# Attention and gated feed-forward on one core: raw weight tiles split at other places, two fetches between write-backs, one rotation a period earlier

## The chip, the cores and the metric

The kernel runs on one core of a Trainium2 chip. The metric is the device time in microseconds of one execution. Engines are named as the profile names them: PE (TensorE; PEld is its weight load), DVE (VectorE), ACT (ScalarE), POOL (GpSimd) and SP (SyncE, which here issues most DMAs). A name with a q behind it, as SPq or ACTq, is the sequencer of that engine issuing a DMA.

## The reference

Four batches of 512 tokens, 512 channels, all float32. The whole is two residual steps:

```
x = x + attn(cond(x, f))        # cond: a two-way decayed scan over the tokens (bi-WKV), gated by x
x = x + ffn(cond2(x, f))        # the same with other decay; ffn: silu(z W1') * (z W3'), Hadamard, W2'
# attn: 16 heads of 128; in segments of 128 tokens: causal softmax(q k') v inside a segment,
# plus sigma(q) mem / (sigma(q) z) from a running memory with delta update, mixed by sigmoid(betas), then Wo
```

The Hadamard transform over the 2048 hidden units is applied to W2 instead (eight blocks), once, while attention runs.

## The kernel before

The attention part is one loop of 32 periods, `for n in range(NN)`, written out for each engine. Period n handles two heads (pair n % 8) of batch n // 8. So the first period is n = 0, the seventh n = 6, the ninth n = 8, the 30th and 31st n = 29 and 30. PE's order in a period is: transposes of the keys, scores, transposes of the output of period n - 1, then pieces of the projections for later periods set between the steps of period n's recurrent memory (`update`, `recall`, `turn_p`, `pv`). The projections are value blocks (`v_block`), used by `couple(n)`, and the keys and queries of period n + 1 (`kq_part`). Every fourth period (n = 4, 8, ...) is a burst that holds Wo (`wo`) besides. After the 32 periods comes the feed-forward, 32 units of `up` and `down`. Every float32 product is three fp32r matmuls (`three`), on high and low parts.

**Weight tiles.** Weights come in an order fixed by `weight_stream()` as numbered tiles, each 1024 columns of a high and 1024 of a low part, in a ring of seven slots (`parts`). ENDS[n] is the number of tiles asked for by the end of period n; ENDS is 4, 6, 10, 12, 24, 28, 32, 34, 46, 50 for n = 0 to 9. A tile that is met for the first time is raw. SP loads its two halves into two of four `stage` buffers (L2450), ACT makes the high part (`split_hi`, L1715) and POOL the low part (`split_w`, L2226); for the q tiles POOL makes both (L2224). `load_w`, `split_hi` and `split_w` take a tile number up to which they go, and all four engines take the calls in their own program order, so a call whose tile has not landed holds everything behind it on its engine. A stage buffer is loaded again when the tile before it in that buffer has been split. Most tiles are written back to HBM after the split (`keep`, L2479 and L2480, 512 KB each) and fetched later, ready (L2467, L2468, in `load_w`). A fetch into a slot waits until the slot's former tile is used, and, if that one was kept, until its write-back has landed (`wait_used`).

Tiles that matter here: 2, 3 = values for period 2 and 3, in n = 0 already; 4 = keys of period 2, 5 = its queries; 28 = keys of period 7, 29 and 30 = values for periods 8 and 9 (computed in period 6), 31 = queries of period 7, 32 = keys of period 8; 40 to 43 = o12 to o15, raw, for Wo of period 8; 44, 45 = keys and queries of period 9; 46, 47 = values computed in period 9, both fetched; 48, 49 = keys and queries of period 10. Tile 46 goes into the slot of tile 39, tile 47 into that of tile 40, tiles 48, 49 and 50 into those of 41, 42 and 43. Period 6 (SWAPPED) takes the first key part of the next period before its value blocks.

**Background steps.** The scans of `cond`, the Hadamard of W2 and so on are a list STEPS with costs, dealt by `shared_out()` to eight slots in each period. `behind(n, k)` on an engine runs its part of the steps of slots up to k. A step of the Hadamard is `load`, four levels `lv0` to `lv3` on DVE, `hi` (ACT, L1789, copies HA to HH), `lo` (DVE, L1246, HL = HA - HH), then `mult`, the rotation: four matmuls of 512 columns on PE (`hadamard`, L880 and L881), whose result ACT scales and sends to HBM (`out_w2`, L1807, L1809). A `mult` goes only into slots 1 to 3, at most one in a slot. PE reaches `behind` at k = 1 (after the first `update`) and k = 3 (after the first `recall`). The steps of the last blocks are dealt so in the kernel before: (29, 1) mult 5; (29, 2) hi 6, lo 6; (29, 3) load 7, lv0 7; (29, 4) lv1; (29, 5) lv2; (29, 7) lv3; (30, 1) mult 6; (30, 2) hi 7, lo 7; (30, 3) mult 7. ACT runs `out_w2(6)` after `hi` 7. The step yh of scan tile 7 (period 6, slot 2: ACT L1781, POOL L2251) completes the input y of batch 1, for which the value block of period 6 waits (`wait_y`).

The waits that gate a value block on PE:

```
if n == 0:
    w.wait_ge(a_qm, 2 + half + 1)          # ACT's relu of the queries of period 1, half
...
elif n == SWAPPED:
    w.wait_ge(a_km, 2 * (n + 1) + half + 1)
```

Of the kernel before, what the change touches and what calls it, by code (L numbers as in the profile page):

```python
# [65 lines left out]
STEPS = [(name, t, cost) for t in range(4, NA) for name, cost in SCAN]  # L66
STEPS += [("hstart", 0, 3000)]
for _i in range(8):
    for name, cost in HADAMARD:
        if name != "mult":  # L70
            STEPS.append((name, _i, cost))
        elif _i > 0:
            if _i == 2:
                STEPS += [(z, 0, c) for z, c in MODULATE[1:]]
            STEPS.append((name, _i - 1, cost))
            if _i == 1:
                STEPS.append(MODULATE[0][:1] + (0, 0))
# [75 lines left out]
SWAPPED = 6  # L153
# [157 lines left out]
def adaln_attn_ffn(nc, xT_d, fT_d, wu_d, wq_d, wk_d, wv_d, wo_d, betas_d,  # L311
# [9 lines left out]
    with ExitStack() as ctx:  # L321
# [1376 lines left out]
        def scalar(e):  # L1698
# [103 lines left out]
            def out_w2(i):  # L1802
                for j in range(2):
                    cut = slice(512 * j, 512 * j + 512)
                    w.wait_ge(pe_h, 2 * i + j + 1)
                    w.wait_ge(d_ho, 16 * i)
                    e.activation(HO[:, cut], X[j][:, :], ACT.Copy, scale=RSQ).then_inc(a_ho, 1)  # L1807
                w.wait_ge(a_ho, 2 * i + 2)
                e.dma_start(w2_s[i].rearrange("p a d -> p (a d)"), HO[:, :]).then_inc(d_ho, 16)  # L1809
# [10 lines left out]
            def behind(n, k):  # L1820
                for name, i, _ in STEPS[at[0]:UPTO[n, k]]:
                    if name == "nf":
                        load_k(i + 2 if i + 2 < NA else NT)
                    elif name == "er":
                        exp_r(i)
                    elif name == "ek":
                        exp_k(after(i))
                    elif name == "eu":
                        exp_u(after(i))
                    elif name == "rc1":  # L1830
                        load_r(i)
                    elif name == "yh":
                        high_y(i)
                        keep_ratio(i)
                    elif name == "hi":
                        high_w2(i)
                        if i == 7:
                            out_w2(6)
                    elif name == "load":
                        load_w2(i)  # L1840
                    elif name == "mult" and i != 6:
                        out_w2(i)
                    elif name == "zsig":
                        z_sigmoid(i)
                    elif name in ("z0", "z1", "z2", "z3"):
                        z_high(i, int(name[1]))
                at[0] = UPTO[n, k]
# [164 lines left out]
            for n in range(NN):  # L2012
                nx, burst = n + 1, is_burst(n)
# [21 lines left out]
                exp_s(n, 1)  # L2035
                behind(n, 1)
                if n in (SWAPPED, NN - 2):
                    copy_kq(nx, "k", 0, G[0])
                    exp_kq(nx, "k", 0, G[0])
                elif more and not bare:  # L2040
                    copy_v(n, 0)
                elif not more:
                    sigmoid(0, 0, G[0])
# [3 lines left out]
                    exp_u(4)  # L2047
                if burst:
                    copy_v(n, 1)
                if n == SWAPPED:  # L2050
                    behind(n, 3)
                split_hi(o + 3 if burst else 3 if n == 0 else end if more else end + 1)
                behind(n, 3)
                if n == SWAPPED:
# [34 lines left out]
                        copy_kq(nx, "k", j, G[j])  # L2089
                        exp_kq(nx, "k", j, G[j])  # L2090
                if more:
                    split_hi(5 if n == 0 else end + (3 if n == 3 else 1 if burst else 2))
                    copy_kq(nx, "q", 0, G[0])
                    exp_kq(nx, "q", 0, G[0])
                    if n not in (0, 4):
                        split_hi(end + (4 if n == 3 else 3 if burst else 2))
                    copy_kq(nx, "q", 1, G[1])
                    if n == 0:
                        exp_kq(nx, "q", 1, G[1])
                    if n == 4:  # L2100
                        split_hi(end + 3)
                else:
                    high_h(0, 0)
                    high_h(0, 1)
# [100 lines left out]
        def gpsimd(e):  # L2205
# [133 lines left out]
            for n in range(NN):  # L2339
# [10 lines left out]
                if n == 0:  # L2350
                    ekv(4)
                    euv(4)
                if n == SWAPPED:
                    behind(n, 3)
                split_w(o + 3 if burst else 3 if n == 0 else end if more else end + 1)
                behind(n, 3)
                if burst:
# [11 lines left out]
                if burst:  # L2369
                    split_w(end + 2)  # L2370
                if more:
                    split_w(5 if n == 0 else end + (4 if n == 3 else 3 if burst else 2))
                else:
                    low_h(0, 0)
                    low_h(0, 1)
# [50 lines left out]
        def sync(e):  # L2426
# [110 lines left out]
            for n in range(NN):  # L2537
# [27 lines left out]
                keep(o + 5 if burst else end + 2 if n == 3 else end)  # L2565
                load_w(o + 9 if burst else 6 if n == 0 else end + (5 if n == 3 else 3))
                behind(n, 5)
                if burst:
                    keep(o + 8)
                    load_w(o + 11)  # L2570
# [5 lines left out]
                    load_w(o + 13)  # L2576
                if more:
                    keep(5 if n == 0 else end + (4 if n == 3 else 2 if burst else 1))
                    load_w(end + (6 if n == 3 else 4))
                behind(n, 7)  # L2580
            def load_x(b):
                w.wait_ge(d_x1[b], 16)
# [107 lines left out]
```

## Time and profile before

| | us |
|---|---|
| median of 3 runs (lowest, highest) | 1588.19 (1587.49, 1588.75) |
| profiled execution, device time | 1588.17 |
| its span | 1586.4 |
| PE busy | 1543.0, 97% |
| DVE busy | 1227.3, 77% |
| ACT busy | 780.6, 49% |
| POOL busy | 614.5, 39% |
| DMA, 42.4% of 16 engines on SP's queue | 276.58 MB |
| mean granted clock of TensorE | 0.997 |

The profiled execution lies 0.02 us under the median, and its time is 1.8 us more than its span. The attention loop starts at 60.71 us of the span and its 32nd period at 1044.61.

### The profile page before, as it was taken

Reading aid. Unit: us, or ns where it says so; the run is one execution under the profiler, and the core shown is the slowest. Engines: PE = TensorE matmul, PEld = TensorE weight load, DVE = VectorE, ACT = ScalarE, POOL = GpSimd, SP = SyncE. Lnnn points to the kernel's source line nnn. Section 1 sums busy time; section 2 is a strip of 40 time slices with the busy share of each in tenths; the row PEclk is TensorE's granted clock in tenths of the full one; section 3 lists DMA queues with packets and bytes.
Section 4 is the critical chain, followed back from the end, with each engine's and each line's share of the span. In section 5 each row is a group of like instructions: output and inputs, shape, how many; then the busy total and the mean of one; then the engine's idle time right before and its main releaser. Section 6 shows DMA issues by size and latency. Waiting matters only on the chain.

```text
span 1586.4 us, 24552 instructions
## 1 busy us (share of the span) xinstructions
PE 1543.0 (97%) x8406; PEld 1323.7 (83%) x8406; DVE 1227.3 (77%) x2746; ACT 780.6 (49%) x1687; POOL 614.5 (39%) x433
## 2 busy tenths in 40 slices
PE   4899999999999999999999999999999999999999
PEld 2678998888888888888888888888888888888887
DVE  8869967897788788888775774666897888687785
ACT  3556655645526535644555562663554443344442
POOL 3647656361211113221101010143664465666662
PEclk9999999999999999999999999999999999999999
DMA  5356677578485387386278658347211122311111
GB/s 176 122 194 242 242 280 255 190 267 316 156 309 186 108 294 246 103 316 236 84 261 338 222 196 311 114 166 260 88 58 54 58 88 74 106 43 64 54 41 54
DMA packets 113405, 276.58 MB, mean 174 GB/s; under 512 B 11648, under 2 KB 36608, under 8 KB 111872
## 3 DMA queue, kind: packets, MB, share of 16 engines
q1 hardware_dynamic: 94416, 241.96, 42.4%
q10 hardware_dynamic: 18864, 33.04, 6.8%
q8 instruction: 68, 1.11, 0.3%
q14 instruction: 57, 0.47, 0.1%
HBM read 226.71 MB, written 48.25 MB: 173 GB/s over the span
## 4 chain that ended last, share of the span: by engine, by line
PE 89%; DVE 5%; issue 2%; ACT 1%; POOL 1%; DMA 1%; SPq 0%; ACTq 0%; POOLq 0%; DVEq 0%
PE psG L664 14%; PE psG L666 14%; PE psG L665 13%; PE psG L788 5%; PE psX L860 3%; PE psX L664 3%; PE psX L666 3%; PE psX L665 3%; PE psX L815 3%; PE psG L790 3%; PE psZ L841 3%; PE psZ L832 2%; PE psZ L666 2%; PE psY L666 2%; PE psZ L665 2%
## 5 line engine op out<-in xcount | busy, mean ns | idle before, releaser
L2226 POOL TENSOR_TENSOR parts<-stage,parts 128x512 fp32r<-128x512 f32 x160 | 234.4, 1487 | 145.2 <-ACT parts L1715 142.9
L664 PE MATMUL psG<-yh,parts 128*128 128x512 f32 x646 | 263.0, 407 | 0.1
L666 PE MATMUL psG<-yh,parts 128*128 128x512 f32 x646 | 253.1, 392 | 0.0
L665 PE MATMUL psG<-yl,parts 128*128 128x512 f32 x646 | 251.9, 390 | 0.0
L2294 POOL TENSOR_TENSOR vs<-v,omb 128x512 f32<-128x512 f32 x64 | 92.0, 1460 | 387.0 <-PE psX L815 209.6
L666 PEld LDWEIGHTS psG<-yh,parts 128*128 128x128 f32 x646 | 121.2, 188 | 26.7
L664 PEld LDWEIGHTS psG<-yh,parts 128*128 128x128 f32 x646 | 121.7, 188 | 22.0 <-issue 0.9
L665 PEld LDWEIGHTS psG<-yl,parts 128*128 128x128 f32 x646 | 121.8, 189 | 21.5
L788 PE MATMUL psG<-heads,parts 128*128 128x512 f32 x384 | 135.5, 394 | 0.0
L1715 ACT ACTIVATE parts<-stage 128x512 fp32r<-128x512 f32 x152 | 87.9, 623 | 56.7 <-DMA stage<-in_w 16.6
L1875 ACT ACTIVATE kT<-psG 128x512 f32<-128x512 f32 x62 | 36.9, 595 | 149.9 <-PE psG L666 148.5
L664 PE MATMUL psG<-parts,yh 128*128 128x512 f32 x240 | 101.8, 424 | 7.8 <-ACT etmp L1893 3.7
L790 PE MATMUL psG<-heads,parts 128*128 128x256 f32 x384 | 108.2, 282 | 0.0
L1220 DVE RECIPROCAL DBK<-DF 128x128 f32<-128x128 f32 x120 | 107.3, 926 | 0.6
L1923 ACT ACTIVATE S<-S,st 128x128 f32<-128x128 f32 x256 | 99.0, 391 | 7.7 <-issue 5.5
L1303 DVE CUSTOM_DVE_ANT_0 S<-psX,mask 128x128 f32<-128x128 f32 x256 | 57.9, 286 | 55.5 <-PE psX L815 55.4
L1315 DVE TENSOR_TENSOR mem<-psZ,mem 128x129 f32<-128x129 f32 x192 | 47.8, 287 | 66.1 <-PE psZ L832 66.1
L666 PE MATMUL psG<-parts,yl 128*128 128x512 f32 x240 | 95.6, 399 | 0.0
L665 PE MATMUL psG<-parts,yh 128*128 128x512 f32 x240 | 94.4, 393 | 0.0
L2302 POOL TENSOR_TENSOR hl<-sg,hh 128x512 fp32r<-128x512 f32 x36 | 51.0, 1416 | 91.0 <-ACT hh L1973 91.0
L788 PEld LDWEIGHTS psG<-heads,parts 128*128 128x128 f32 x384 | 72.1, 188 | 14.7
L1884 ACT ACTIVATE etmp<-etmp 128x512 f32<-128x512 f32 x126 | 79.5, 632 | 3.9
(281 smaller groups left out, 4146.3 us busy)
## 6 DMA issues: line engine op xcount, KB each, us to landing
parts<-high_o SPq DMA_DIRECT2D x52, 512.0 KB, 6.0
parts<-low_o SPq DMA_DIRECT2D x52, 512.0 KB, 7.5
parts<-high_v SPq DMA_DIRECT2D x36, 512.0 KB, 5.2
parts<-low_v SPq DMA_DIRECT2D x36, 512.0 KB, 6.4
stage<-in_w SPq DMA_DIRECT2D x64, 256.0 KB, 3.1
parts<-high_k SPq DMA_DIRECT2D x23, 512.0 KB, 5.6
parts<-low_k SPq DMA_DIRECT2D x23, 512.0 KB, 7.0
parts<-high_q SPq DMA_DIRECT2D x23, 512.0 KB, 4.9
```

The lines of the kernel that those rows point to most:

```text
L664: e.matmul(out, lh, rh, start=first, stop=False, skip_group_check=check)
L665: e.matmul(out, lh, rl, start=False, stop=False, skip_group_check=check)
L666: return e.matmul(out, ll, rh, start=False, stop=last, skip_group_check=check)
L788: e.matmul(out[:, :], hi[:, cols], heads[:, :, 8 * half + r, :], start=half == 0 and r == 0, stop=last_row, skip_group_check=True)
L790: k = e.matmul(out[:, 0:256], lo[:, cols], heads[:, 0, 8 * half + r, :], start=False, stop=last_row, skip_group_check=True)
L1220: e.reciprocal(dbk[:, 128 * j:128 * j + 128], df[:, 128 * j:128 * j + 128]).then_inc(v_rc, 1)
L1303: m = e.tensor_tensor_reduce(S[:, j, seg(s)], X[j][:, seg(s)], mask[:, :], -SCALE, -NEG, ALU.add, ALU.min, st[:, 1, j, s:s + 1])
L1715: e.activation(hi, raw, ACT.Copy).then_inc(a_wh, 1)
L1884: e.activation(below(n, kind, j), below(n, kind, j), ACT.Exp, scale=-1.0).then_inc(a_ke if kind == "k" else a_qe, 1)
L1923: m = e.activation(S[:, j, seg(s)], S[:, j, seg(s)], ACT.Exp, bias=st[:, 1, j, s:s + 1], scale=-1.0, accum_out=st[:, 2, j, s:s + 1])
L2226: e.tensor_tensor(lo, raw, hi, ALU.subtract).then_inc(p_wl, 1)
L2294: e.tensor_tensor(vs[:, :, j, :].rearrange("p (a b) d -> p a b d", a=2), pick(v[:, :, :, j, 0:P], *HALVES[n]), omb[:, 128 * j:128 * j + 12 ...
```

## The change

1. n = 0, ACT: `split_hi(5)` (tile 4) stands behind the copies and exponentials of the queries of period 1, no longer ahead of them.
2. n = 5: ACT and POOL also split tile 30 at the end of the period (`end + 3` for `end + 2`), and SP also loads tile 32 there (`end + 5` for `end + 4`). They did the one inside period 6's softmax (`end - 1`) and the other at the start of period 6.
3. n = 6 and n = 30, ACT: `behind(n, 2)` runs ahead of the copy and the exponential of the next keys, not behind them. In n = 6 `behind(n, 3)` no longer stands ahead of the split of tile 31, on ACT and POOL.
4. n = 8, SP: the fetches of tiles 46 and 47 are set between the write-backs: write back 40, fetch 46, write back 41, fetch 47, write back 42 and 43. Before, 40 to 43 were written back and then 46 and 47 fetched.
5. Rotation 6 is one period up. The list now deals: (29, 3) mult 6; (29, 4) load 7, lv0 7; (29, 5) lv1; (29, 6) lv2; (29, 7) lv3; (30, 1) nothing; (30, 2) hi 7, lo 7; (30, 3) mult 7. `out_w2(6)` runs with it, in (29, 3).

```diff
--- before.py
+++ after.py
@@ -66,10 +66,12 @@
 STEPS = [(name, t, cost) for t in range(4, NA) for name, cost in SCAN]
 STEPS += [("hstart", 0, 3000)]
 for _i in range(8):
+    if _i == 7:
+        STEPS.append(("mult", 6, 300))
     for name, cost in HADAMARD:
         if name != "mult":
             STEPS.append((name, _i, cost))
-        elif _i > 0:
+        elif 0 < _i < 7:
             if _i == 2:
                 STEPS += [(z, 0, c) for z, c in MODULATE[1:]]
             STEPS.append((name, _i - 1, cost))
@@ -1834,11 +1836,9 @@
                         keep_ratio(i)
                     elif name == "hi":
                         high_w2(i)
-                        if i == 7:
-                            out_w2(6)
                     elif name == "load":
                         load_w2(i)
-                    elif name == "mult" and i != 6:
+                    elif name == "mult":
                         out_w2(i)
                     elif name == "zsig":
                         z_sigmoid(i)
@@ -2035,6 +2035,7 @@
                 exp_s(n, 1)
                 behind(n, 1)
                 if n in (SWAPPED, NN - 2):
+                    behind(n, 2)
                     copy_kq(nx, "k", 0, G[0])
                     exp_kq(nx, "k", 0, G[0])
                 elif more and not bare:
@@ -2047,8 +2048,6 @@
                     exp_u(4)
                 if burst:
                     copy_v(n, 1)
-                if n == SWAPPED:
-                    behind(n, 3)
                 split_hi(o + 3 if burst else 3 if n == 0 else end if more else end + 1)
                 behind(n, 3)
                 if n == SWAPPED:
@@ -2089,16 +2088,17 @@
                         copy_kq(nx, "k", j, G[j])
                         exp_kq(nx, "k", j, G[j])
                 if more:
-                    split_hi(5 if n == 0 else end + (3 if n == 3 else 1 if burst else 2))
+                    if n > 0:
+                        split_hi(end + (3 if n == 3 else 1 if burst else 2))
                     copy_kq(nx, "q", 0, G[0])
                     exp_kq(nx, "q", 0, G[0])
                     if n not in (0, 4):
-                        split_hi(end + (4 if n == 3 else 3 if burst else 2))
+                        split_hi(end + (4 if n == 3 else 3 if burst or n == 5 else 2))
                     copy_kq(nx, "q", 1, G[1])
                     if n == 0:
                         exp_kq(nx, "q", 1, G[1])
-                    if n == 4:
-                        split_hi(end + 3)
+                    if n in (0, 4):
+                        split_hi(5 if n == 0 else end + 3)
                 else:
                     high_h(0, 0)
                     high_h(0, 1)
@@ -2350,8 +2350,6 @@
                 if n == 0:
                     ekv(4)
                     euv(4)
-                if n == SWAPPED:
-                    behind(n, 3)
                 split_w(o + 3 if burst else 3 if n == 0 else end if more else end + 1)
                 behind(n, 3)
                 if burst:
@@ -2369,7 +2367,7 @@
                 if burst:
                     split_w(end + 2)
                 if more:
-                    split_w(5 if n == 0 else end + (4 if n == 3 else 3 if burst else 2))
+                    split_w(5 if n == 0 else end + (4 if n == 3 else 3 if burst or n == 5 else 2))
                 else:
                     low_h(0, 0)
                     low_h(0, 1)
@@ -2565,6 +2563,10 @@
                 keep(o + 5 if burst else end + 2 if n == 3 else end)
                 load_w(o + 9 if burst else 6 if n == 0 else end + (5 if n == 3 else 3))
                 behind(n, 5)
+                if n == 8:
+                    load_w(o + 11)
+                    keep(o + 6)
+                    load_w(o + 12)
                 if burst:
                     keep(o + 8)
                     load_w(o + 11)
@@ -2576,7 +2578,7 @@
                     load_w(o + 13)
                 if more:
                     keep(5 if n == 0 else end + (4 if n == 3 else 2 if burst else 1))
-                    load_w(end + (6 if n == 3 else 4))
+                    load_w(end + (6 if n == 3 else 5 if n == 5 else 4))
                 behind(n, 7)
             def load_x(b):
                 w.wait_ge(d_x1[b], 16)
```

## Rows read from the trace of the kernel before

**Rows 1.** Waits of PE, whole span (total us, times, longest us):
```profile
PE psG L664 <- ACT etmp L1893: 3.7, 1, 3.7
PE psG L664 <- POOL yl L2251: 2.5, 1, 2.5
...
PE psG L664 <- issue: 1.7, 1, 1.7
...
PE psX L880 <- DVE HL L1246: 1.3, 1, 1.3
```

**Rows 2.** Busy time by stretch, one period each (us, PE, PEld, DVE, ACT, POOL, clock):
```profile
60.71:93.18 32.47, 27.82 (x151) 23.30 (x151) 20.73 (x59) 18.84 (x46) 25.13 (x21) 0.95 0.64 214
93.18:119.26 26.08, 26.08 (x160) 22.95 (x158) 20.57 (x63) 16.67 (x41) 9.71 (x8) 1.00 0.39 137
248.47:278.91 30.44, 27.95 (x159) 24.12 (x158) 22.23 (x63) 16.55 (x41) 18.04 (x15) 0.94 0.78 276
353.54:381.53 27.99, 26.34 (x160) 23.02 (x159) 22.21 (x65) 15.63 (x39) 6.90 (x5) 1.00 0.99 390
993.58:1020.61 27.03, 27.03 (x164) 23.75 (x163) 19.50 (x62) 16.05 (x39) 2.56 (x2) 1.00 0.38 135
```

**Rows 3.** The same view of two short stretches:
```profile
87.30:90.70 3.40, 3.40 (x10) 2.62 (x9) 0.00 (x0) 1.36 (x3) 1.84 (x3) 0.50 1.01 346
356.90:358.70 1.80, 0.14 (x3) 0.06 (x1) 1.80 (x11) 1.56 (x6) 0.05 (x1) 1.00 1.04 418
```

**Rows 4.** Timeline of PE at two waits inside the loop (start, us, what, idle before):
```profile
81.95 0.39 PE L666 MATMUL psG<-yh,parts 128*128 128x512 f32 x1
86.02 0.47 PE L664 MATMUL psG<-parts,yh 128*128 128x512 f32 x1 [3.68 <-ACT etmp L1893]
...
261.31 0.72 PE L664 MATMUL psG<-parts,yh 128*128 128x512 f32 x1 [2.49 <-POOL yl L2251]
```

**Rows 5.** Timeline of ACT, end of the first period:
```profile
83.23 0.63 ACT L1715 ACTIVATE parts<-stage 128x512 fp32r<-128x512 f32 x1 [5.00 <-DMA stage<-in_wk]
84.27 0.63 ACT L1715 ACTIVATE parts<-stage 128x512 fp32r<-128x512 f32 x1 [0.41 <-DMA stage<-in_wk]
...
85.28 0.59 ACT L1893 ACTIVATE etmp<-psG 128x512 f32<-128x512 f32 x1
```

**Rows 6.** Timelines of ACT and of POOL in the seventh period:
```profile
254.48 1.14 ACT L1715 ACTIVATE parts<-stage 128x512 fp32r<-128x512 f32 x2
...
257.07 0.57 ACT L1875 ACTIVATE kT<-psG 128x512 f32<-128x512 f32 x1
...
258.69 0.61 ACT L1781 ACTIVATE yh<-OY 128x512 fp32r<-128x512 f32 x1
...
259.38 1.68 POOL L2251 TENSOR_TENSOR yl<-OY,yh 128x512 fp32r<-128x512 f32 x1 [0.64 <-ACT yh L1781]
```

**Rows 7.** SP in the ninth period: an issue, its waits, landing of L2468 at 343.53:
```profile
343.17 0.32 SPq L2467 DMA_DIRECT2D parts<-high_v  x1
...
SPq L2467 <- DMA low_o<-parts: 7.0, 4, 2.5
...
DMA to landing us min/median/max: 15.1/15.1/15.1
```

**Rows 8.** Timelines of PE, DVE and ACT, 30th and 31st period:
```profile
1003.21 0.47 PE L664 MATMUL psG<-parts,yh 128*128 128x512 f32 x1
...
1003.81 1.22 DVE L1246 TENSOR_TENSOR HL<-HA,HH 128x1024 fp32r<-128x1024 f32 x1 [3.04 <-ACT HH L1789]
...
1027.73 0.58 ACT L1875 ACTIVATE kT<-psG 128x512 f32<-128x512 f32 x1
...
1029.37 1.04 ACT L1789 ACTIVATE HH<-HA 128x1024 fp32r<-128x1024 f32 x1
...
1030.44 1.23 DVE L1246 TENSOR_TENSOR HL<-HA,HH 128x1024 fp32r<-128x1024 f32 x1 [2.65 <-ACT HH L1789]
...
1031.77 0.47 PE L880 MATMUL psX<-HH,had 128*128 128x512 f32 x1 [1.28 <-DVE HL L1246]
```

## The prediction

> **What bounds the kernel now.** I read the page's busy times first: PE works for 97% of the span, so only two things can move the end, PE's work or PE's waits. The edits add and remove no work on any engine; they move it. So next come PE's waits. Inside the loop there are four of more than 1 us [rows 1], and the change has a part for each: 3.7 us for ACT's relu of the queries, 2.5 for a low part of y from POOL, 1.7 that the profile can't name, and 1.3 for HL from DVE. Then I cut the loop into periods. An ordinary one takes 26.08 us, all of it PE; the first, seventh and ninth take 32.47 (with other work in it), 30.44 and 27.99 [rows 2]. The seventh is 4.36 longer but idle for 2.5 only. The rest is the clock: after the long idle stretch of the first period PE was granted 0.50, the 1.2 GHz level, for 3.4 us [rows 3], and matmuls of 512 columns that are otherwise 0.23 us apart (the pace of the whole timeline) come 0.43 apart; the seventh period has the same, mean clock 0.94 [rows 2]. The 1.66 us wait at 357 us did not lower it, 1.00 all through [rows 3]. After the loop the change touches nothing.
>
> **First period (part 1).** PE's last query matmul starts at 81.95, the first of the value block at 86.02 [rows 4]. It waited for the relu at 85.28, 0.59 long [rows 5]. ACT was idle for 5.00 us before that, in its program order stuck at the split of tile 4, whose halves land at 83.2 and 84.3 [rows 5]. The queries of head 0 were ready at about 79.7 (12 matmuls of 0.23 before PE's end). After the change ACT takes copy and relu then and is done by 81, before PE gets there at 82.18; head 1's relu is done by 83.5, while PE needs it 12 matmuls later, at 84.9. Gain: 86.02 - 82.18 = 3.84, and of the half-clock stretch half of 3.4 = 1.7, together 5.5. What is late instead: tile 4's split starts at about 84.0 rather than 83.23, so its low part on POOL is 0.8 later. It is used only in the middle of period 1, over 10 us later. With the cover gone (if POOL's later split of tile 5 then held period 1's queries) it would cost what POOL is late, 0.8.
>
> **Seventh period (parts 2 and 3).** PE's wait ends with yl, 259.38 + 1.68 = 261.06 on POOL, 0.25 before PE's start at 261.31 [rows 4, 6]. yl waits for yh, which ACT starts at 258.69, and ahead of yh stand, in this period, the split of tile 30 (1.14 of two, 1.05 net) and the copy, relu and exponential of the next keys, 258.69 - 257.07 = 1.62 [rows 6]. Both leave: yh starts at 258.69 - 1.05 - 1.62 = 256.02, ends 256.63; POOL, without tile 30's 3.5 us, starts yl at 256.71 and ends by 258.39, and PE may go at 258.64. PE's natural start is 261.31 - 2.49 - 0.17 (the modelled overlap) = 258.65. So the wait goes just to nothing. The keys' relu, which this block also needs, ends at about 257.7. Gain: all that this period has over an ordinary one, 30.44 - 26.08 = 4.36 [rows 2], idle and half clock. The split goes to the end of period 5, on ACT between the two heads' queries, where its 1.05 us delays the second copy by 0.15, and on POOL behind tile 29, well before yh. SP's extra load waits there for POOL's low part of tile 30, and the write-back of tile 29 is queued behind it, some 2.5 us later; nobody needs that slot before period 8. Bounds: 0.5 less if yl is late again, nothing more.
> The Trainium skill (SBUF — State Buffer, "SBUF: two separate sides") says that a VectorE operation with two SBUF inputs and a GpSimd one that reads SBUF exclude each other for a whole instruction. By it yl, moved beside a scan, would wait for that scan; the sum would be 0.5 smaller. The row's 1.68 for yl is already such a slow one, so the sum above stands by the row.
>
> **Ninth period (part 4).** PE starts again at 358.67; the fetch of tile 47's low half is issued at 343.53 and lands 15.1 later, at 358.63 [rows 7]. That is the unnamed wait. SP issued this fetch at 343.17, just when the write-back of tile 40 had landed (its waits are of this kind, 7.0 us of four) [rows 7]. From then on ten halves land in 15.5 us: six of write-backs 41 to 43, two of tile 46, two of 47, so 1.55 each at a full DMA (share 1.04) [rows 3]. After the change tile 47 still can't be issued before 343.17, but ahead of it are only 41 and 46: six halves, 9.3 us, landing at 352.5. PE needs it at 358.67 - 1.66 - 0.17 = 356.8. Gain: 27.99 - 26.08 = 1.91 [rows 2]. Late instead: write-backs 42 and 43, and behind them tiles 48 to 50; the keys (48) stay the 11th and 12th halves, 343.1 + 18.6 = 361.7, needed at 353.54 + 10.1 = 363.6 (in an ordinary period those keys' first matmul lies 10.1 in). Cover is thin, 1.9 us.
>
> **Rotation (part 5, and part 3 in n = 30).** Here the change pays. In (29, 3) PE has finished the recall and starts its next work at 1003.21 [rows 8]. Rotation 6 now stands there, and it needs HL of block 6, which DVE makes from 1003.81 to 1005.03, right behind ACT's HH, and neither moves [rows 8]. With the 0.1 us that PE took after HL at 1031.67 [rows 8], PE starts at 1005.12: a new wait of 1.9. The rotation's own work, about 27.03 - 26.08 = 0.95 [rows 2], only changes its period. In period 30 HL of block 7 held PE until 1031.77; the natural start, at the same place as 1003.21 in its period (9.63 after 993.58), is 1020.61 + 9.63 = 1030.24, so 1.53 is lost now. After the change HH starts at 1027.73, without the keys' 1.64 ahead of it, HL ends 1.04 + 0.02 + 1.23 later at 1030.02, PE could go at 1030.12, but it arrives 0.95 earlier, at 1029.29: 0.83 is still lost. Net: 1.91 - 1.53 + 0.83 = +1.21. Levels of block 7 are one slot later; the one in slot 6 puts DVE's sigma of the keys about 1 us nearer to the next period, with 2 us of room. ACT's wait for the w2 write ahead of its second output goes, and hides nothing for PE.
>
> **Sum.** -5.5 - 4.4 - 1.9 + 1.2 = -10.6 on the span of 1586.4: 1575.8. The device time of this execution is 1.8 above its span, 1588.17, at the median of 1588.19. I predict 1577.5, by 0.67% faster. Its own range is 1576.5 to 1578.5.
>
> **Rivals.**
> - *The new wait in period 29 lowers the clock.* Idle 1.7 us there is as long as the wait at 357 us that left it at 1.00 [rows 3], against it. For it: two longer ones did lower it. Price half of 3.4 = 1.7, time 1579.2. The Trainium skill (TensorE: Matmul & The Clock Gate, "What's actually happening") says that the gate goes by how busy the engine has lately been; by it either level is possible, which is why this has a chance.
> - *The rotation finds HL ready*, if ACT or DVE come to hi 6 and lo 6 sooner than the rows show. Then 1.9 of the sum goes: 1575.6. Nothing in the diff moves them, against it.
> - *The seventh period keeps part of its wait.* yl is ready at PE's natural start to within 0.01. If ACT is held at tile 30 in period 5, or yl starts late, idle and perhaps the clock come back: 0.5 to 4.4, time 1578 to 1581.9.
> - *The early gain is given back.* PE comes to periods 1 to 3 5.5 us sooner, and DVE, POOL (25.13 of 32.47 busy) or a load may not be [rows 2]. Against: ACT and POOL idle in period 1, POOL busy 9.71 of 26.08. Time up to 1583.
> - *The parts do nothing*: the relu is not what held PE, tile 47 isn't either. Against: both releases fit to 0.2 us. Time 1588.2.
> - *Slower: SP stands still at tile 47.* In period 8 everything behind (42, 43, 48, 49, 50) waits for one write-back. If its landing slips, tile 48 lands after 363.6 and PE stalls in period 9. To lose more than the other parts gain (8.7 without the 1.9, and 3.2 more to be slower by 0.2%), it would have to land at 363.6 + 8.7 + 3.2 = 375.5, 13.8 later than worked out. Nine more halves would do that. Time 1591.4 and up.
>
> **Chances.** Main case 0.60, clock 0.11, HL ready 0.08, seventh period 0.08, given back 0.06, nothing 0.04, slower 0.03. A difference under 0.2%, 3.2 us, is about what a measurement of this kernel can't tell from none. The range 1575.0 to 1582.0 takes in the first four, 0.87. Faster by over 0.2% (below 1585.0): the first five, 0.93; within: 0.04; slower: 0.03.
>
> **What the profile after would show.** In the first period no wait of PE for ACT's etmp, and clock 1.00 where it was 0.50; period length near 26.9. In the seventh, L2251 at about 248 + 8.2 after the shift of 5.5, no wait, 26.1 long. In the ninth, 26.1 long, fetch of tile 47 landing 4 us ahead of use, SP's L2467 between L2479 and L2480 pairs. In the 30th, PE waiting about 1.7 idle for DVE HL L1246, the period 29.9 long; in the 31st, another of 0.6, 22.3 long instead of 24.0. I would be wrong if one of the three large gains is matched by a longer period next to it, or if the clock falls at a place where it didn't.

## The result and the profile after

The changed kernel takes 1578.13 us (median of 6 runs, 1577.67 to 1582.11), the kernel before 1587.84 beside it (6 runs, 1585.40 to 1588.75). The ratio is 0.9945, with a 95% interval of 0.9933 to 0.9958: faster by 0.4 to 0.7%. The prediction was 1577.5.

The first profiled execution was the longest of the six. TensorE was granted 0.95 of full speed in nearly all of it. So I also read a second one, from the run `after_again` below: 1578.28 us, clock 0.998. Both pages, first and second execution; the columns are busy us, share of the span and instructions:

```profile
span 1580.3 us, 24552 instructions
...
PE 1544.1 (98%) x8406; PEld 1326.8 (84%) x8406; DVE 1227.1 (78%) x2746; ACT 780.9 (49%) x1687; POOL 614.9 (39%) x433
```

```profile
span 1576.4 us, 24552 instructions
...
PE 1539.6 (98%) x8406; PEld 1321.4 (84%) x8406; DVE 1228.8 (78%) x2746; ACT 780.5 (50%) x1687; POOL 614.9 (39%) x433
```

Everything below reads the second, whose clock is like that of before. Its span is 9.93 below the 1586.4 of before. First PE's waits, as in [rows 1] (us in total, times, longest):

```profile
...
PE psX L882 <- issue: 2.3, 2, 1.7
PE psG L679 <- DVE qT L1208: 1.6, 1, 1.6
PE psZ L842 <- DVE mem L1317: 1.3, 4, 0.5
```

The four waits of [rows 1] are gone from the list. In their place stand two of the rotation (L882 is L880 of before; PE's lines are two further down), 1.7 and 0.6, and one of 0.5 for `mem`. Then the periods, as in [rows 2]: first, second, seventh, ninth, 30th and 31st (us, PE, PEld, DVE, ACT, POOL, clock, DMA share, GB/s):

```profile
60.42:87.33 26.91, 25.95 (x151) 22.25 (x151) 20.77 (x60) 19.10 (x46) 21.40 (x17) 1.00 0.55 192
87.33:114.16 26.83, 26.35 (x160) 22.91 (x159) 21.35 (x63) 16.66 (x41) 13.81 (x12) 1.00 0.60 203
243.38:269.48 26.10, 26.10 (x160) 22.99 (x159) 22.13 (x63) 15.85 (x40) 17.62 (x15) 1.00 0.84 285
344.16:370.26 26.10, 26.10 (x160) 22.99 (x159) 22.14 (x65) 15.52 (x39) 6.87 (x5) 1.00 1.02 401
982.26:1012.08 29.82, 28.14 (x168) 24.56 (x167) 19.44 (x62) 17.13 (x41) 2.56 (x2) 1.00 0.41 139
1012.08:1034.43 22.35, 21.76 (x140) 19.31 (x139) 15.68 (x54) 16.75 (x41) 8.06 (x6) 1.00 0.13 36
```

Lengths before and after, with the difference: first 32.47, 26.91 (-5.56); second 26.08, 26.83 (+0.75); seventh 30.44, 26.10 (-4.34); ninth 27.99, 26.10 (-1.89); 30th 27.03, 29.82 (+2.79); 31st 24.00, 22.35 (-1.65). Together -9.90 of the -9.93. The windows are cut at PE's first matmul of each period. The period that the prediction calls the ninth, at 353.54 in before, is that of n = 9, the tenth if one counts from the first. It is called the ninth here too. SP issues the transfers for it in the period ahead of it, n = 8.

The first period, ACT's rows against [rows 5] and PE's against [rows 4]:

```profile
79.84 0.59 ACT L1893 ACTIVATE etmp<-psG 128x512 f32<-128x512 f32 x1
...
83.95 1.24 ACT L1717 ACTIVATE parts<-stage 128x512 fp32r<-128x512 f32 x2
```

```profile
81.66 0.39 PE L668 MATMUL psG<-yh,parts 128*128 128x512 f32 x1
81.89 0.39 PE L666 MATMUL psG<-parts,yh 128*128 128x512 f32 x1
```

The relu is done at 80.4, and PE goes from the last query matmul to the value block with the usual 0.23 between. The split of tile 4 now starts at 83.95.

The seventh, ACT and POOL against [rows 6]:

```profile
250.96 0.61 ACT L1783 ACTIVATE yh<-OY 128x512 fp32r<-128x512 f32 x1
251.48 0.57 ACT L1875 ACTIVATE kT<-psG 128x512 f32<-128x512 f32 x1
```

```profile
251.65 1.32 POOL L2251 TENSOR_TENSOR yl<-OY,yh 128x512 fp32r<-128x512 f32 x1 [4.31 <-ACT yh L1783]
```

The step yh lies 7.6 us into the period, where it was 10.2, ahead of the copy of the keys, and yl follows with 1.32 rather than 1.68. A scan of DVE was still going when yl began:

```profile
250.67 1.21 DVE L1169 TENSOR_TENSOR_SCAN DF<-dec,EK 128x512 f32<-128x512 f32 x1
```

SP in n = 8, against [rows 7] (SPq L2465 and L2466 are fetches, L2477 and L2478 write-backs):

```profile
323.77 0.55 SPq L2477 DMA_DIRECT2D high_o<-parts  x1
...
325.20 0.65 SPq L2465 DMA_DIRECT2D parts<-high_v  x1
...
326.73 0.66 SPq L2477 DMA_DIRECT2D high_o<-parts  x1
...
333.88 0.32 SPq L2465 DMA_DIRECT2D parts<-high_v  x1
...
334.91 0.42 SPq L2477 DMA_DIRECT2D high_o<-parts  x1
...
339.29 0.32 SPq L2465 DMA_DIRECT2D parts<-high_k  x1
```

In order: write-back 40, fetch 46, write-back 41, fetch 47, write-backs 42 and 43, fetch 48. The halves of tile 47 land at 340.06 and 341.92. PE comes to the value block at about 347.4, 5.5 later.

The rotation in the 30th and the 31st period, PE and DVE, against [rows 8]:

```profile
991.76 0.39 PE L843 MATMUL psZ<-mem,sq 128*128 128x129 f32 x2
993.82 0.47 PE L882 MATMUL psX<-HH,had 128*128 128x512 f32 x1 [1.68 <-issue]
...
1021.62 0.47 PE L882 MATMUL psX<-HH,had 128*128 128x512 f32 x1 [0.59 <-issue]
```

```profile
992.50 1.22 DVE L1248 TENSOR_TENSOR HL<-HA,HH 128x1024 fp32r<-128x1024 f32 x1 [3.04 <-ACT HH L1791]
```

HL ends at 993.72 and PE starts 0.10 later. The profile calls it "issue", but the end of HL fits; rotation_hi_early below tests it.

### The profile page after: what moved, and what is told of

It is laid out like the page before. It is cut to its first block, busy times and chain, and to the rows that moved or that the text cites. A ratio compares the mean times of both kernels' runs of the same rounds, so it can differ in the third digit from the quotient of the medians.

```text
span 1580.3 us, 24552 instructions
## 1 busy us (share of the span) xinstructions
PE 1544.1 (98%) x8406; PEld 1326.8 (84%) x8406; DVE 1227.1 (78%) x2746; ACT 780.9 (49%) x1687; POOL 614.9 (39%) x433
## 3 DMA queue, kind: packets, MB, share of 16 engines
q8 instruction: 68, 1.11, 0.3%
## 4 chain that ended last, share of the span: by engine, by line
PE 91%; DVE 5%; issue 2%; ACT 1%; POOL 0%; DMA 0%; ACTq 0%; SPq 0%; DVEq 0%; POOLq 0%
PE psG L666 14%; PE psG L668 14%; PE psG L667 14%; PE psG L790 6%; PE psX L862 4%; PE psX L666 3%; PE psX L668 3%; PE psX L667 3%; PE psX L817 3%; PE psG L792 3%; PE psZ L843 3%; PE psZ L834 3%; PE psZ L842 2%; PE psZ L668 2%; PE psY L668 2%
```

## The experiments

Theory A is the prediction's: five parts worth -5.5, -4.4, -1.9 and, for the rotation with its order on ACT, +1.2, which add up because they lie in different periods. Its rivals: the rotation costs nothing or its wait isn't HL's; the parts don't add up; and, once the trace of after was read, the second period's 0.75 belongs to something else than part 1. All times are medians in us where there were more runs, with the profiled span and the lengths of the periods n = 0, 1, 6, 9, 29 and 30:

| kernel | time (runs) | span | 0 | 1 | 6 | 9 | 29 | 30 |
|---|---|---|---|---|---|---|---|---|
| before | 1587.88 (13) | 1586.4 | 32.47 | 26.08 | 30.44 | 27.99 | 27.03 | 24.00 |
| after_again | 1578.40 (4) | 1576.4 | 26.91 | 26.83 | 26.10 | 26.10 | 29.81 | 22.35 |
| no_rotation | 1576.13 (4) | 1574.3 | 26.91 | 26.62 | 26.10 | 26.10 | 27.03 | 22.95 |
| rotation_only | 1590.85 (10) | 1590.3 | 33.73 | 26.11 | 30.45 | 27.96 | 29.82 | 23.97 |
| rotation_hi_early | 1578.12 (1) | 1576.3 | 26.90 | 26.59 | 26.10 | 26.10 | 29.37 | 22.36 |
| first_only | 1582.42 (1) | 1580.6 | 26.89 | 26.67 | 30.46 | 27.70 | 27.03 | 24.03 |
| fetch_only | 1582.71 (1) | 1580.9 | 30.84 | 26.07 | 28.85 | 26.10 | 27.03 | 24.02 |
| split_only | 1586.62 (1) | 1584.8 | 32.88 | 26.09 | 27.45 | 27.47 | 27.03 | 24.01 |
| order_only | 1584.12 (1) | 1582.3 | 32.44 | 26.07 | 27.73 | 27.75 | 27.03 | 22.95 |
| rotations_later | 1576.08 (4) | 1574.2 | 26.90 | 26.61 | 26.10 | 26.10 | 27.03 | 22.96 |
| rotation_later_29 | 1577.32 (1) | 1575.5 | 26.89 | 26.60 | 26.10 | 26.10 | 27.93 | 22.35 |
| before_look1 | 1587.54 (1) | 1585.7 | 32.39 | 26.08 | 28.85 | 28.16 | 27.03 | 23.99 |
| before_look2 | 1590.08 (1) | 1588.3 | 32.63 | 26.07 | 30.42 | 29.89 | 27.03 | 24.00 |

The periods of "before" are those of the trace shown ahead of the prediction; its 13 runs were made beside the first four experiments, the second to fifth row (1585.73 to 1590.39). The four single parts had one run of before beside them (1587.49), the last four rows seven (median 1586.48, 1585.29 to 1591.13). A single time can't tell parts of 1 to 3 us from the spread of before, so the single parts are judged by their periods.

**after_again.** The changed kernel as it is.

> The changed kernel as it is, run again. Its first profiled execution was granted a clock of 0.949 all through and took 1582.1 us, while five others took 1577.7 to 1578.8 at 0.996 to 0.998. Theory: the 0.949 belongs to that execution and not to the kernel, so this profile has 1.00 again, a span near 1576.2, periods of 26.1 us (not 26.25), the 30th period near 29.8 and the 31st near 22.3. Rival: the changed kernel is throttled now and then because TensorE is busier; then 0.95 shows again here.

Measured: 1578.40 (1578.28 to 1578.55), ratio 0.9933 (0.9918 to 0.9948), clock 0.998 or 0.999 in all four runs. So the long first execution is not what the kernel usually does. It is one of ten of the changed kernel. The rival, that the change makes such an execution likelier, is neither borne out nor excluded by these runs.

**no_rotation.** Without part 5, all else as after.

```diff
-    if _i == 7:
-        STEPS.append(("mult", 6, 300))
...
-        elif 0 < _i < 7:
+        elif _i > 0:
...
                         high_w2(i)
+                        if i == 7:
+                            out_w2(6)
...
-                    elif name == "mult":
+                    elif name == "mult" and i != 6:
```

> The changed kernel with its part 5 undone: rotation 6 is back in the 31st period, while ACT still copies HH ahead of the next keys there. Theory (the rotation put one period up costs 1.2 us, and the earlier HH is what helps): the 30th period is 27.0 us without a wait for HL, the 31st 22.5 with a wait of at most 0.2, since HL ends at 9.4 into the period and PE reaches rotation 7 at 9.6. Together 49.5 for 52.4 in the changed kernel: 2.9 us less, 1575.2 us in all. Rival (the rotation put up is what removes the wait in the 31st period): the wait of 1.3 there comes back, the two periods take 51.0 and the time is 1.4 us less than the changed kernel's; if moving it up was a gain by itself, the time is above 1578.

Measured: 1576.13 (1575.95 to 1577.04), ratio to before 0.9920 (0.9905 to 0.9935), 2.3 below after_again on the same chip. Period 29 is 27.03 again, and period 30 is 22.95, not the 22.5 that I expected. The timeline of ACT has the reason, and PE's the rest (start, us, what, idle before and who ended it):

```profile
1017.06 1.06 ACT L1789 ACTIVATE HH<-HA 128x1024 fp32r<-128x1024 f32 x1 [0.47 <-PE psX L881]
```

```profile
1019.48 0.47 PE L880 MATMUL psX<-HH,had 128*128 128x512 f32 x1 [0.24 <-DVE HL L1246]
```

There is one HH. Its copy for block 7 has to wait until rotation 6, in the same period, has read it. Moving rotation 6 out of period 30 frees HH sooner and takes PE's work with it, which is worth 0.60 there (22.95 against 22.35). But it costs 2.79 in period 29.

**rotation_only.** Part 5 alone on the kernel before (the same lines the other way round).

> The kernel before with part 5 alone. Theory: the 30th period gets the wait for HL of block 6, idle 1.7 us, and is 29.9 long; in the 31st PE comes 0.95 earlier to rotation 7 while HL of block 7 still stands behind the keys on ACT, so it ends as late in the period as before and the period stays near 24.0 with a wait of 2.2. Sum 53.9 for 51.0: 2.9 us slower than before, 1590.9 us. Clock 1.00 in both waits, or 1.7 more if a 2.2 us wait lowers it. Rival (the rotation alone is worth its part): not slower than before.

Measured: 1590.85 (1589.96 to 1595.26), ratio 1.0021 (1.0011 to 1.0030): slower by 3.0. Period 29 is 29.82 as in after, and period 30 gains nothing (23.97): without part 3, ACT's HH still comes behind the keys, so PE, earlier by the rotation's work, only waits longer:

```profile
1035.10 0.47 PE L882 MATMUL psX<-HH,had 128*128 128x512 f32 x1 [2.21 <-issue]
```

The shorter period 30 of after needs both parts, and the -1.65 there is mostly part 3's: order_only alone has 22.95.

**rotation_hi_early.** In period 29 ACT makes HH of block 6 ahead of a copy of values, so that HL, and nothing else of PE's, comes earlier.

```diff
                 elif more and not bare:
+                    if n == 29:
+                        behind(n, 2)
                     copy_v(n, 0)
```

> The changed kernel, and in the 30th period ACT makes HH of block 6 ahead of the copy of a value block (0.5 us) instead of behind it. Theory (PE waits there for HL, that is for ACT's HH): the wait falls by 0.5, from 1.67 to about 1.2, the period from 29.8 to 29.3. Rival (PE waits for the bank or for the output of rotation 5, or for nothing that moves): 29.8 as in the changed kernel.

Measured: PE's wait is 1.20 instead of 1.68, and the period 29.37 instead of 29.81.

```profile
993.26 0.47 PE L882 MATMUL psX<-HH,had 128*128 128x512 f32 x1 [1.20 <-issue]
```

PE's wait moves with HL, by 0.48, while PE's own work before it stays. So what the profile calls "issue" is HL, as the prediction had it.

**first_only, fetch_only, split_only, order_only.** One part each on the kernel before, in this order: part 1; part 4; part 2; part 3.

```diff
-                    split_hi(5 if n == 0 else end + (3 if n == 3 else 1 if burst else 2))
+                    if n > 0:
+                        split_hi(end + (3 if n == 3 else 1 if burst else 2))
...
-                    if n == 4:
-                        split_hi(end + 3)
+                    if n in (0, 4):
+                        split_hi(5 if n == 0 else end + 3)
```

```diff
+                if n == 8:
+                    load_w(o + 11)
+                    keep(o + 6)
+                    load_w(o + 12)
```

```diff
-                        split_hi(end + (4 if n == 3 else 3 if burst else 2))
+                        split_hi(end + (4 if n == 3 else 3 if burst or n == 5 else 2))
...
-                    load_w(end + (6 if n == 3 else 4))
+                    load_w(end + (6 if n == 3 else 5 if n == 5 else 4))
```

(the first of these also in `split_w` for POOL)

```diff
                 if n in (SWAPPED, NN - 2):
+                    behind(n, 2)
                     copy_kq(nx, "k", 0, G[0])
...
-                if n == SWAPPED:
-                    behind(n, 3)
```

(the second of these also for POOL)

> The kernel before with part 1 alone (ACT splits tile 4 behind the queries of period 1). Theory: the first period falls from 32.47 to 26.8 us, with no stretch at clock 0.50 behind it, the periods 1 to 5 keep their lengths, time 5.6 us less, 1582.4. Rival (the gain is given back): one of the next periods grows by as much as PE comes early, up to 5.5 us in all.

> The kernel before with part 4 alone (fetches of tiles 46 and 47 between the write-backs). Theory: the ninth period's follower, n = 9, falls from 27.99 to 26.1 us; tile 47 is still asked for only at 343.2, when the write-back of tile 40 has landed, but lands at about 352.5 rather than 358.6. Time 1.9 us less. Rival (the DMA engines are full, so later transfers are late instead): PE waits in the same period for the keys, tile 48, and the period stays above 27.

> The kernel before with part 2 alone (tile 30 split and tile 32 loaded one period earlier). Theory: in the seventh period (n = 6) yh still stands behind the keys on ACT but 1.05 us earlier, at about 257.6; yl ends at about 260.0 and PE goes at 260.2, 1.6 us late instead of 2.65; the idle time is then 1.4, too short to lower the clock. The period is 27.7 us for 30.44. Rival (all of the wait goes already with the tile off POOL): 26.1. Rival (the tile was not in the way): 29.4 or more.

> The kernel before with part 3 alone (background steps ahead of the keys' copy in n = 6 and n = 30). Theory for n = 6: ACT starts yh at about 257.07, but POOL is at the low part of tile 30 until 258.74 and makes yl then, to 260.4; PE goes at 260.7, 2.0 us late, idle 1.85, clock 1.00; the period is 28.1 us. For n = 30: HL of block 7 is there before PE, the wait of 1.3 goes, the period falls from 24.0 to 22.5. Rival: yl waits for more than ACT's order, and n = 6 stays above 29.

first_only: period 0 is 26.89 and period 1 26.67 instead of 26.08, the others as before but for the ninth, 27.70, whose wait varies. (The time, 1582.42, is the 1582.4 expected by luck: the expectation had no give-back, and the loop of this execution started 0.68 earlier.) So the give-back in period 1 belongs to part 1. PE's longer period 1 has one place. In the second trace of after its matmuls lie as before, to 0.01, up to the end of the first `update`'s projections; the first `recall` starts 0.63 later in the period, ends 0.11 later still, and all that follows stays 0.75 behind. PE, DVE and POOL there:

```profile
95.86 0.49 PE L842 MATMUL psZ<-mem,sk 128*128 128x129 f32 x2 [0.48 <-DVE mem L1317]
```

```profile
90.82 1.47 DVE L1375 SCALAR_TENSOR_TENSOR sq<-qT,etmp 128x512 f32<-128x512 f32 x1
92.22 1.28 DVE L1361 TENSOR_TENSOR heads<-psY,heads 128x512 fp32r<-128x512 f32 x2
93.42 0.68 DVE L1375 SCALAR_TENSOR_TENSOR sq<-qT,etmp 128x512 f32<-128x512 f32 x1
94.02 0.41 DVE L1143 TENSOR_SCALAR EK<-kx 128x512 f32<-128x512 f32 x1
94.35 1.27 DVE L1195 TENSOR_TENSOR_SCAN NBK<-dec,last,NF 128x512 f32<-128x512 f32 x1
95.54 0.46 DVE L1317 TENSOR_TENSOR mem<-psZ,mem 128x129 f32<-128x129 f32 x2
```

```profile
90.45 1.29 POOL L2226 TENSOR_TENSOR parts<-stage,parts 128x512 fp32r<-128x512 f32 x1
```

DVE goes from 90.82 to `mem` without a gap, so what makes its first step longer makes PE late. That step, sq, took 1.47, its twin at 93.42 0.68. In before this step took 0.69. There the same POOL instruction ended at 93.30, 3.4 ahead of sq; here it ends at 91.74, with sq begun. In six traces with part 1 the long sq (1.25 to 1.47) ends 0.55 after that POOL instruction, each time: 92.29 after 91.74, 91.74 after 91.19, 92.11 after 91.55. A step slowed by sharing would not end so. It stood still until POOL was done. PE's loss follows it: in these six traces sq is 0.56 to 0.78 longer than in before, and the period, each time, 0.02 to 0.05 less than that. By the Trainium skill (SBUF — State Buffer, "SBUF: two separate sides") a VectorE operation with two SBUF inputs and a GpSimd one that reads SBUF hold their port one at a time; the trace agrees here. I didn't run a kernel that takes POOL's split away from there, so that the 0.6 to 0.8 of sq is what reaches PE rests on the rows.

fetch_only: period 9 is 26.10, all of part 4's 1.89. But periods 0 and 6 are 1.6 shorter than before, with PE's waits still there. This was unexpected, and before_look1 and before_look2 below are there to explain it. By the other traces without part 4 in which the clock stays up there (27.47 to 28.16), it is worth 1.4 to 2.1.

split_only and order_only: either alone leaves a wait of PE in the seventh period, 1.11 and 1.40, and a period 1.35 and 1.63 longer than an ordinary one. The clock stayed at 1.00 there. POOL's rows, split_only and order_only:

```profile
258.69 1.27 POOL L2251 TENSOR_TENSOR yl<-OY,yh 128x512 fp32r<-128x512 f32 x1 [5.98 <-ACT yh L1781]
```

```profile
255.22 3.46 POOL L2225 TENSOR_TENSOR parts<-stage,parts 128x512 fp32r<-128x512 f32 x2 [5.35 <-ACT parts L1715]
258.65 1.26 POOL L2250 TENSOR_TENSOR yl<-OY,yh 128x512 fp32r<-128x512 f32 x1
```

In split_only yl waits for ACT, which had the keys first. In order_only ACT is in time, but POOL is held by tile 30. Each of the two parts takes one of them away. Both periods are shorter than expected (27.7 and 28.1), in order_only by what yl is shorter: no scan was ahead of it, and it took 1.26 and not the 1.68 of before. Period 30 of order_only is 22.95 and not 22.5, for the reason found in no_rotation.

**rotation_later_29.** After, with the rotation of period 29 twelve projection matmuls later on PE.

```diff
                 recall(n, 1)
-                behind(n, 3)
+                if n != 29:
+                    behind(n, 3)
...
+                if n == 29:
+                    behind(n, 3)
                 turn_p(n)
```

> The changed kernel, and in the 30th period PE does rotation 6 behind 12 more matmuls of the projections (2.8 us later in its order). Theory (the cost of part 5 is only the place, where HL isn't there): no wait, the period is 27.03 + 0.95 = 28.0 for 29.8, the 31st as before at 22.35, time 1.8 less than the changed kernel, 1576.5. Rival (two rotations in a period cost more than their matmuls, through the bank or through the output's wait for HO): PE waits elsewhere in the period, which stays above 28.5.

Measured: period 29 is 27.93, and PE has no wait at the rotation (994.87, right behind 994.64). So the +2.79 of period 29 is the rotation's work, 0.9, and 1.88 of waiting for HL. The time of this one run, 1577.32, is 1.1 below after_again and not 1.9: its loop starts 0.4 later (60.85 for 60.42), and what follows the loop took 492.7 rather than 491.9.

**rotations_later.** no_rotation, with the second rotation of period 30 behind `turn_p` on PE.

```diff
-                behind(n, 3)
+                if n != NN - 2:
+                    behind(n, 3)
...
                 turn_p(n)
+                if n == NN - 2:
+                    behind(n, 3)
```

> The version without part 5 (1576.1 us), and in the 31st period PE does rotation 7 behind the transposes of the scores instead of ahead of them. In that version the period is 22.95 us and PE still waits 0.5 for HL, since ACT's HH of block 7 has to wait until rotation 6 has read the one before. Theory: with 0.9 us of other work in front, the wait is covered and the period is 22.5; 0.45 less in all, 1575.7, which is under what the medians can tell. Rival: ACT's output of the rotation now stands in front of its copy of the transposed scores at the wrong time, PE waits for that instead, and the period stays at 22.95 or grows.

Measured: 1576.08 (1575.25 to 1576.39), ratio 0.9931 (0.9912 to 0.9950), period 30 22.96: nothing gained. My theory, that the wait for HL was all that period 30 had left to give, fell. PE now stands a little later for ACT:

```profile
1023.65 1.60 PE L860 MATMUL psX<-vs,pT 128*128 128x128 f32 x12 [0.24 <-ACT pT L1934]
```

The wait of 0.24 for HL in no_rotation is one of 0.24 for the transposed scores here.

**before_look1, before_look2.** The kernel before, unchanged, twice.

> The kernel before, for its granted clock. In its first trace the clock fell to half for 3.4 us behind both long waits; in the trace with part 4 alone the same two waits were 3.6 and 2.5 us long and the clock did not fall, the periods were 30.84 and 28.85 us instead of 32.47 and 30.44. Theory: the fall is drawn anew in each execution and is worth 1.6 us each time, so the periods are one or the other of these values, and the spread of this kernel's times (1585.4 to 1590.4) holds it. Rival: part 4 itself kept the clock up; then this run has both falls, 32.5 and 30.4.

> The same kernel once more, a second draw: by the theory either value in each of the two periods, by the rival 32.5 and 30.4 again.

PE's clock behind the waits; first fetch_only (behind the wait of the first period, 3.65, and of the seventh, 2.51), then before_look1 (behind 3.64 and 2.50), then before_look2 (behind the 1.94 of the ninth):

```profile
85.50:89.00 3.50, 3.50 (x15) 2.88 (x16) 0.00 (x0) 2.64 (x5) 1.33 (x3) 1.00 0.92 363
259.20:262.60 3.40, 3.40 (x21) 3.00 (x22) 0.64 (x4) 1.09 (x2) 3.23 (x4) 1.00 1.03 401
```

```profile
85.80:89.20 3.40, 3.40 (x9) 2.64 (x10) 0.00 (x0) 2.54 (x5) 1.15 (x3) 0.50 0.93 364
261.10:264.50 3.40, 3.40 (x21) 2.99 (x22) 0.69 (x5) 1.09 (x2) 3.23 (x4) 1.00 0.99 386
```

```profile
360.10:363.40 3.30, 3.30 (x10) 2.62 (x10) 0.00 (x0) 1.69 (x7) 0.62 (x1) 0.50 1.02 394
```

With the clock at 1.00 PE gets 15 to 21 instructions done in 3.4 us, at 0.50 nine or ten. The same wait of the same kernel is followed by the 1.2 GHz level in one execution and not in another. In the seven traces that have the first period's wait of 3.6 to 4.1, the clock fell behind it in six (not in fetch_only). Of the six with the seventh's 2.5, it fell in four (not in fetch_only and before_look1). Each fall makes its period 1.6 longer: 30.44 against 28.85 in the seventh, 32.47 against 30.84 in the first.

## Why the prediction was right, and where it was off

**First period.** -5.5 predicted, -5.56 measured. PE goes straight on, the split of tile 4 starts at 83.95 (84.0 predicted). The 3.9 of it that is idle stretch is saved in every execution; the 1.6 of the clock only in those in which it would have fallen.

**Seventh.** -4.4, measured -4.34, no wait. "The wait goes just to nothing" had the value of yl at 1.68; it took 1.32, and yh came at 7.6 where I had 7.55. Both parts are needed for it. The prediction weighed at 0.5 that yl has to stand still for a scan of DVE. It does, and it costs almost nothing here: yl ended 1.09 after the scan (251.88), and as the scan had only 0.23 left, that made 1.32 of it. In before the scan had 0.6 left, and yl ended 1.06 after it, with 1.68; without a scan ahead it takes 1.26 or 1.27 (order_only, split_only). So the row's 1.68 was the slow case, as the prediction said.

**Ninth.** -1.9, measured -1.89. Tile 47 is 5.5 ahead of its use (4.3 predicted, from 1.55 a half), SP went on with tile 48 when 41's write-back had landed, and 48 was in time: its halves landed by 351.51, PE needs them 10.1 into the period, at about 354.3. The slower rival did not come.

**Rotation.** +1.2, measured +1.14: +2.79 in the 30th (1.9 and 0.95 predicted, 1.88 and 0.9 measured), -1.65 in the 31st (-1.53 + 0.83 - 0.95 = -1.65 predicted). The clock did not fall at this wait, in after_again nor at the 2.21 in rotation_only. Against the kernel that has all other parts the rotation costs 2.3, more than the 1.2, as part of what period 30 gains comes from part 3 alone.

**The term that was mis-sized** is the give-back, which the sum had at nothing: "against: ACT and POOL idle in period 1". It was 0.75 (0.5 to 0.75 in the traces with part 1). The prediction looked at how busy POOL is over period 1, 9.71 of 26.08, and not at where: POOL's last work of period 0 came only 1.6 us sooner (90.45 for 92.01) while PE came to period 1 5.85 sooner, so it slid into the first 4.5 us of period 1, where one DVE step needs the same port. The rival had the right sign and place and 0.06 of the chance; its price was small enough to leave the forecast standing. The 0.8 that the prediction names as its cover for this part is near the 0.75 by chance: that was for POOL's split holding period 1's queries, which did not happen.

**The sum.** Predicted -10.6 on the span, measured -9.93; the 0.75 explains it. The time came out at 1578.13 (1578.40 in the second set) for 1577.5.

**Treated as certain, and not so:** the 1.7 each for the clock in the first and seventh period. They were in this execution of before, so the sum against it is right. But before has executions without them. That fits its spread, 1585.29 to 1591.13, against 0.3 for the four of after_again and 1.1 for the first six without the long one. Without the two falls its span would be 1586.4 - 1.6 - 1.6 = 1583.2 and the gain 6.8; against before_look2, with all three falls, it is 11.9. A part of what this change gives is that the waits behind which the clock may fall are gone. That the forecast came within 0.6 us rests in part on luck: the execution it was read from had two of the three falls and lay at the median of its set.

**The best version** is no_rotation: parts 1 to 4 without the fifth, 1576.13, 0.8% below before, and 2.3 below the change as made. rotations_later, 1576.08 in other company, is by its periods not different from it.

## What to carry to other kernels

Price each edit in the period where its wait ends last, and then look at what the neighbours of that period had going on at that moment of time, not over the period: work that doesn't move with the bottleneck engine slides against it. Moving a unit of work of the bound engine forward is free only if its operands are there: compare the end of the producer with the new place, row by row, and, where they don't fit, put the unit behind other ready work (rotation_later_29) or leave it. A part of a change that pays can hide one that costs, so time the change without each part.

## What the runs showed of the hardware

**Whether the clock falls behind a wait is not settled by the wait.** It fell behind 6 of 7 waits of 3.6 to 4.1 us, behind 4 of 6 of 2.5, and behind one (1.94) of the twenty of 1.1 to 2.2 us in these traces; 1.83 and 2.21 are among those it did not fall behind. Each fall lasts 3.4 us (in rotation_only once 6.8) and costs 1.6.

**A whole execution at 0.95.** In the first trace of after the granted clock is 0.95 from about 25 us to the end, but for 6.8 us at 0.50 ahead of the loop. The three rows: its seventh period, its last 491.6 us, and the same stretch of before at 1.00:

```profile
244.18:270.46 26.28, 26.28 (x159) 23.13 (x158) 22.14 (x63) 15.84 (x40) 17.66 (x15) 0.95 0.82 287
1088.60:1580.20 491.60, 487.43 (x2150) 403.00 (x2148) 377.34 (x482) 213.84 (x325) 285.55 (x183) 0.95 0.22 70
```

```profile
1094.70:1586.30 491.60, 487.41 (x2150) 402.83 (x2148) 378.09 (x482) 213.73 (x325) 284.44 (x183) 1.00 0.22 70
```

In the feed-forward part, whose matmuls have 512 columns, windows of the same length hold the same 2150 matmuls, with PE's busy time within 0.02, at 0.95 and at 1.00. The attention periods, with matmuls of 128 and 129 columns among them, took 0.1 more each on average (26.28 against 26.10 in the seventh). The loop up to the 32nd period is 3.3 longer and starts 0.7 later, where the 6.8 us at 0.50 lie; with 0.1 less behind, that is the 3.9 us by which this span exceeds 1576.4. So 5% of clock cost 0.3% of the loop's time and nothing measurable behind it. At 0.50 the 512-column matmuls start 0.427 apart, so by the clock alone they would be 0.214 apart at 1.00 and 0.225 at 0.95 (an estimate from that one pace). They are 0.227 apart at both, so it is not the clock that sets their pace there; what does, no run shows. What brought the level on stays open; it was not seen in the other 13 traces.

**DVE and POOL standing still for each other.** The six long sq are not the only ones. In the trace of before sq takes 0.68 or 0.69 where POOL is idle (46 times); the 16 begun while a TENSOR_TENSOR of POOL ran took 0.97 to 1.50, and each ended 0.55 after POOL's. Scans with two SBUF inputs (L1167, L1170) take 1.16 to 1.23 alone and took 1.24 to 2.29 in 17 such cases, each ending 1.08 after POOL's. It goes the other way too: all seven yl of POOL begun under such a scan took 1.45 to 2.02 and ended 1.06 to 1.10 after it. A DVE step that reads PSUM (x from x and psZ) kept its 0.68 in all 21 cases beside POOL. The profile shows the standing still as a longer instruction and not as idle time, so it is found by comparing an instruction with its twins.
